# Convolution columns with the feature ahead of the distance, the ternary weights in 48 even pieces, and the squares moved to GpSimd

## What is computed

```python
# k = v = context, q = layer-normed x; 32 heads of head_dim 8, L = 512
kv = jnp.einsum('bhil,bhjl->bijhl', k_, v_)
y = jnp.fft.irfft(jnp.fft.rfft(kv, n=2*L) * jnp.fft.rfft(ssm_kernel, n=2*L), n=2*L)[..., :L]
out = y + kv * D[None, None, None, :, None]
out = jnp.einsum('bijhl,bhil->bjhl', out, q_)
...
def weight_quant(w):
    scale = 1.0 / jnp.clip(jnp.mean(jnp.abs(w)), EPS, None)
    return jnp.clip(jnp.round(w * scale), -1.0, 1.0) / scale
```

## Time and profile before

| | |
|---|---|
| median of 3 runs | 736.14 us (735.43 to 736.41) |
| the profiled execution | 736.74 us, of which its span 734.9 us |
| PE busy | 635.0 us, 86% |
| DVE busy | 556.8 us, 76% |
| ACT busy | 440.3 us, 60% |
| POOL busy | 265.3 us, 36% |
| attention | 0 to 296.3 us |
| convolution with ternary weights | 296.3 to 457 us |
| convolution without them | 457 to 489 us |
| last heads and first rows of the feed-forward part | 489 to 507 us |
| feed-forward part | 507 to 734.9 us |

### The profile page before, as it was taken

The page is one execution under the profiler, slowest core; times in us unless marked ns, Lnnn a source line. Parts: engine busy times, 40 slices in busy tenths (PEclk is TensorE's granted clock), DMA queues, the critical chain, the costliest instruction groups (busy, mean ns, idle before and its releaser), DMA issues.

```text
span 734.9 us, 10711 instructions
## 1 busy us (share of the span) xinstructions
PE 635.0 (86%) x3055; PEld 354.8 (48%) x3074; DVE 556.8 (76%) x981; ACT 440.3 (60%) x751; POOL 265.3 (36%) x248
## 2 busy tenths in 40 slices
PE   5899999999999988877778787974789999999995
PEld 3435454554545434655556565652344444444442
DVE  3465756767583644488787888999999999999983
ACT  2446675676667551666666666421676767767781
POOL 1001010000100030555554555642565655656672
PEclk9969999999999969999999999995999999999998
DMA  9535072543618150444535544220001011010001
GB/s 315 143 136 116 1 229 50 178 100 128 171 57 229 44 143 0 153 159 132 181 118 148 170 130 124 85 86 15 15 16 58 29 43 43 29 57 29 15 30 43
DMA packets 34245, 72.51 MB, mean 99 GB/s; under 512 B 4336, under 2 KB 16112, under 8 KB 32560
## 3 DMA queue, kind: packets, MB, share of 16 engines
q1 hardware_dynamic: 31056, 60.72, 28.0%
q10 hardware_dynamic: 3168, 11.54, 4.9%
HBM read 47.51 MB, written 4.28 MB: 70 GB/s over the span
## 4 chain that ended last, share of the span: by engine, by line
DVE 26%; issue 11%; ACT 9%; POOL 6%; PE 5%; ACTq 1%; DVEq 1%; POOLq 0%
POOL big L790 6%; DVE qo L758 4%; ACT wst L848 4%; DVE toep L1184 3%; DVE xq L1170 3%; DVE mb L1188 3%; PE ps L1061 2%; PE ps L1049 2%; DVE act8t L1220 2%; ACT wt L852 2%; ACT ys L829 2%; DVE x_all L1133 1%; DVE mx L1155 1%; DVE xn L1151 1%; DVE st L1138 1%
## 5 line engine op out<-in xcount | busy, mean ns | idle before, releaser
L705 PE MATMUL ps<-kv,toep 128*128 128x288 f32 x640 | 165.4, 416 | 35.5 <-DVE big L750 33.5
L705 PEld LDWEIGHTS ps<-kv,toep 128*128 128x128 f32 x640 | 121.4, 193 | 79.6 <-issue 47.7
L1061 PE MATMUL ps<-wt,xqt 128*128 128x512 bf16 x496 | 122.1, 389 | 11.1 <-DVE toep L1184 9.5
L758 DVE TENSOR_REDUCE qo<-big 128x2048 f32 (+1 forms) x32 | 124.2, 3881 | 0.0
L1313 POOL TENSOR_TENSOR big<-toep,wst 128x512 f32<-128x512 f32 x64 | 81.6, 1276 | 59.5 <-DVE toep L1184 59.4
L393 ACT ACTIVATE big<-ps,kscale 128x512 f32<-128x512 f32 x128 | 85.2, 696 | 13.6 <-PE ps L243 11.9
L243 PE MATMUL ps<-qx,kx 128*128 128x512 f32 x128 | 78.2, 639 | 11.2 <-ACT big L393 10.4
L790 POOL TENSOR_TENSOR big<-ys,qd 128x768 f32<-128x768 f32 x32 | 55.4, 1732 | 85.9 <-ACT ys L830 68.6
L1061 PEld LDWEIGHTS ps<-wt,xqt 128*128 128x128 bf16 x512 | 48.6, 100 | 67.0 <-DVE toep L1184 11.2
L747 DVE TENSOR_TENSOR big<-ps,qd 128x1024 f32<-128x1024 f32 x32 | 39.1, 1223 | 38.2 <-ACT ys L830 37.3
L1049 PE MATMUL ps<-wt,act8t 128*128 128x512 bf16 x253 | 60.8, 386 | 7.8 <-DVE act8t L1220 7.7
(11 more groups left out here) (121 smaller groups left out, 1011.8 us busy)
## 6 DMA issues: line engine op xcount, KB each, us to landing
qx<-kv SPq DMA_DIRECT2D x128, 128.0 KB, 2.4
wst<-in_wall SPq DMA_DIRECT2D x12, 1024.0 KB, 6.0
wst<-in_wall ACTq DMA_DIRECT2D x22, 512.0 KB, 4.6
toep<-krows SPq DMA_DIRECT2D x32, 256.0 KB, 3.4
ctx<-in_ctxt SPq DMA_DIRECT2D x32, 192.0 KB, 2.4
out_y<-ot SPq DMA_DIRECT2D x16, 256.0 KB, 2.0
conv_part<-qo SPq DMA_DIRECT2D x14, 256.0 KB, 2.7
x_all<-in_x SPq DMA_DIRECT2D x2, 1536.0 KB, 14.4
```

The lines of the kernel that those rows point to most:

```text
L705: mm = pe.matmul(m.ps[:, LB * r + lb, :].rearrange("p (b s) -> p b s", s=WIDE)[:, :, 0:PAIRS], m.toep[r][:, d * P:(d + 1) * P], m.kv[r][:, ...
L758: nc.vector.tensor_reduce(qo[:, :, bass.ds(h * HD, HD)], z[r].rearrange("p n s j -> p n j s"), AX.X, ALU.add).then_inc(s_red.sem, 1)
L1061: mm = pe.matmul(bank[:, n % 2, :], xqt[r][:, k, :], wt[:, k, n * C:(n + 1) * C], start=(k == 0), stop=(k == CK - 1))
```

## The change

Four things change together.

1. The columns of `kv` and so of the convolved sums are ordered with the feature first and the distance second: column 4 i + d in place of 8 d + i. POOL writes the products with a step of 4 numbers, ACT gathers with a step of 4 out of PSUM, and `z` is laid out as block[feature][shift], so that the sum reads consecutive numbers. DVE then writes runs of 4 (line 747) and single numbers with a step of 8 (line 750), and POOL writes with a step of 8 in `multiply_shifted`.
2. POOL makes the squares too: its first instruction for a head's products covers distances 0 to 3 (1024 numbers per partition in place of 768). ACT's squares are gone.
3. The weights come in 48 pieces of 512 columns, three in each of the 16 turns of two heads. In the even head's part the first piece stands between `empty` and `double`, the second behind `double`; in the odd head's the third stands between `empty` and `double`.
4. The pieces are loaded by SP, with three buffers (`wst` has four slots, of which the fourth only serves the later load of `g`). The first stage reads the same array in four pieces for each load.

```diff
-def context_products(nc, m, r, first):
+def context_products(nc, m, r):
 
     c, kv = m.ctx[r][:], m.kv[r].rearrange("p l (b s) -> p (l b) s", s=PAIRS)
-    n = HD // 2 - first
-    whole = nc.gpsimd.tensor_tensor(kv[:, :, first * HD:HD * HD // 2].rearrange("p n (d i) -> p n d i", i=HD),
-                                    window(c, 0, (CW, LB * B), (0, n), (1, HD)),
-                                    window(c, first, (CW, LB * B), (1, n), (1, HD)), ALU.mult)
...
+    n = HD // 2
+    nc.gpsimd.tensor_tensor(window(kv, 0, (PAIRS, LB * B), (1, n), (n, HD)),
+                            window(c, 0, (CW, LB * B), (0, n), (1, HD)),
+                            window(c, 0, (CW, LB * B), (1, n), (1, HD)), ALU.mult)
     return nc.gpsimd.tensor_tensor(kv[:, :, HD * HD // 2:PAIRS], c[:, :, 0:HD // 2], c[:, :, HD // 2:HD], ALU.mult)
...
-        nc.vector.tensor_tensor(z[r][:, :, 0:H, :],
-                                y[:, :, 0:H * HD].rearrange("p n (d j) -> p n d j", j=HD),
-                                window(q, 0, (2 * HD, NB), (1, H), (1, HD)), ALU.mult)
-        nc.vector.tensor_tensor(z[r][:, :, H, :].rearrange("p n (a j) -> p n a j", j=H),
+        nc.vector.tensor_tensor(z[r][:, :, :, 0:H],
+                                y[:, :, 0:H * HD].rearrange("p n (j d) -> p n j d", d=H),
+                                window(q, 0, (2 * HD, NB), (1, HD), (1, H)), ALU.mult)
+        nc.vector.tensor_tensor(z[r][:, :, :, H].rearrange("p n (a j) -> p n a j", j=H),
...
-        nc.vector.tensor_reduce(qo[:, :, bass.ds(h * HD, HD)], z[r].rearrange("p n s j -> p n j s"), AX.X, ALU.add).then_inc(s_red.sem, 1)
...
+        nc.vector.tensor_reduce(qo[:, :, bass.ds(h * HD, HD)], z[r][:], AX.X, ALU.add).then_inc(s_red.sem, 1)
...
         with sp.Fori(1, PR - 1) as i:
-            for r in range(2):
-                toeplitz(i, r)
-                context(i + 1, r)
+            toeplitz(i, 0)
+            context(i + 1, 0)
+            toeplitz(i, 1)
+            weights(i, 0)
+            weights(i, 1)
+            context(i + 1, 1)
+            weights(i, 2)
...
-            nc.gpsimd.tensor_tensor(z[r][:, :, HD - SHIFTS:HD, :],
+            nc.gpsimd.tensor_tensor(z[r][:, :, :, HD - SHIFTS:HD].rearrange("p n j s -> p n s j"),
...
-            y = sums(r)[:, :, HD:H * HD].rearrange("p n (d i) -> p n d i", i=HD)
+            y = sums(r)[:, :, 0:H * HD].rearrange("p n (i d) -> p n d i", d=H)[:, :, 1:H, :]
...
+        def turn(i, first=False):
+            for r in range(2):
+                empty(2 * i + r, r, first)
+                ternary(i, 2 * r)
+                double(2 * i + r + 2, r)
+                if r == 0:
+                    ternary(i, 1)
 
         for r in range(2):
             double(r, r, first=True)
...
+        turn(0, first=True)
+        with act.Fori(1, PR - 1) as i:
+            turn(i)
         for r in range(2):
             empty(H2 - 2 + r, r)
+        for s in range(3):
+            ternary(PR - 1, s)
```

More of the change, by code:

```diff
@@ L50 @@
 WCH = 12
+PIECES = WCH * FF // C
 LN_EPS, RMS_EPS, SUB_EPS, Q_EPS = 1e-5, 1.1920929e-07, 1e-6, 1e-5
@@ L177, in _ @@
         for r in range(2):
-            sp.dma_start(wst[:, r, :], wall[r]).then_inc(d_ws[r].sem, 16)
+            sp.dma_start(wst[:, r, :].rearrange("p (b n) -> p b n", n=C),
+                         wall[r * 4:(r + 1) * 4].rearrange("b p n -> p b n")).then_inc(d_ws[r].sem, 16)
         spread_q(1)
@@ L580, in weight_means @@
             dve.wait_ge(c_scale.sem, 1)
-            nc.vector.tensor_copy(m.wscale.rearrange("p (w k) -> p w k", w=3), spread(wrec[:], WCH // 3))
+            nc.vector.tensor_copy(m.wscale.rearrange("p (w k) -> p w k", w=3), spread(wrec[:], PIECES // 3))
         def turn(i, has_prev=True, has_next=True, rows=True):
@@ L729, in convolve @@
     qd = [sb(f"qd{r}", [P, NB, 2, HD]) for r in range(2)]
-    z = [m.big[:, (2 + r) * FF:(3 + r) * FF].rearrange("p (n i j) -> p n i j", i=HD, j=HD) for r in range(2)]
-    d_wc = [sig("d_wc0"), sig("d_wc1")]
+    z = [m.big[:, (2 + r) * FF:(3 + r) * FF].rearrange("p (n j s) -> p n j s", j=HD, s=HD) for r in range(2)]
+    d_wc = [sig(f"d_wc{s}") for s in range(3)]
     s_ys, s_qd, s_z1, s_z2, s_red = (sig(n) for n in ("s_ys", "s_qd", "s_z1", "s_z2", "s_red"))
-    s_sq = m.s_sq
     s_rnd, s_tern = sig("s_rnd"), sig("s_tern")
@@ L771, in context, with weights @@
             sp.wait_ge(m.s_kv.sem, 2 * i + r - 1)
-            sp.wait_ge(s_sq.sem, 2 * i + r - 1)
             load_context(sp, m, ctxt, 2 * i + r, r)
-        for r in range(2):
-            load_weights(sp, 0, r)
-        with sp.Fori(1, PR - 1) as i:
-            for r in range(2):
-                toeplitz(i, r)
-                context(i + 1, r)
+        def weights(i, s, first=False):
+            if not first:
+                sp.wait_ge(s_tern.sem, 3 * i + s - 2)
+            sp.dma_start(wst[:, s, :], wall[bass.ds(3 * i + s, 1)].rearrange("o p n -> (o p) n")
+                         ).then_inc(d_wc[s].sem, 16)
+        for s in range(3):
+            weights(0, s, first=True)
+        with sp.Fori(1, PR - 1) as i:
+            toeplitz(i, 0)
[5 more added lines that the diff above has]
+            weights(i, 2)
         for r in range(2):
             toeplitz(PR - 1, r)
+        for s in range(3):
+            weights(PR - 1, s)
     def gpsimd(pool):
@@ L842, in double, with ternary @@
                      ).then_inc(s_qd.sem, 1)
-        def ternary(n, r):
-            act.wait_ge(d_wc[r].sem, (n + 1) * 16)
+        def ternary(i, s):
+            n = 3 * i + s
+            act.wait_ge(d_wc[s].sem, (i + 1) * 16)
             apart(act)
-            act.activation(wst[:, r, :], wst[:, r, :], ACT.Identity, bias=m.magic[:, 0:1],
+            act.activation(wst[:, s, :], wst[:, s, :], ACT.Identity, bias=m.magic[:, 0:1],
                            scale=m.wscale[:, bass.ds(n, 1)]).then_inc(s_rnd.sem, 1)
-            act.wait_ge(s_rnd.sem, 2 * n + r + 1)
+            act.wait_ge(s_rnd.sem, n + 1)
             apart(act)
[L852 to L857, removed]
+            act.activation(wt[:, bass.ds(n, 1), :].rearrange("p o n -> p (o n)"),
+                           wst[:, s, :], ACT.Sign, bias=m.magic[:, 1:2]).then_inc(s_tern.sem, 1)
+        def turn(i, first=False):
[5 more added lines that the diff above has]
+                    ternary(i, 1)
         for r in range(2):
             double(r, r, first=True)
[L861 to L876, removed]
-                squares(2 * i + r + 2, r, i + 2)
-                double(2 * i + r + 2, r)
+        turn(0, first=True)
+        with act.Fori(1, PR - 1) as i:
+            turn(i)
         for r in range(2):
             empty(H2 - 2 + r, r)
+        for s in range(3):
+            ternary(PR - 1, s)
     def vector(dve):
@@ L1043, in down @@
         def down(t, first=False):
-            if not first:
+            if first:
+                pe.wait_ge(m.s_tern.sem, PIECES)
+            else:
                 wait(pe, s_fin, t - 1, 1)
@@ L1371, in decoder_layer @@
         m.d_toep = [Signal(ctx.enter_context(nc.semaphore(f"d_toep{r}")), 16) for r in range(2)]
-        m.s_kv, m.s_sq, m.s_conv = (Signal(ctx.enter_context(nc.semaphore(n)), 1) for n in ("s_kv", "s_csq", "s_conv"))
+        m.s_kv, m.s_conv = (Signal(ctx.enter_context(nc.semaphore(n)), 1) for n in ("s_kv", "s_conv"))
         with ExitStack() as stage:
```

28 lines of the change are left out of this document (10 added, 18 removed).

## The result

The median fell from 736.26 us (735.43 to 736.41, 4 runs) to **689.31 us** (688.91 to 690.51, 4 runs): a ratio of 0.9367, interval 0.9351 to 0.9383. The profiled execution took 688.91 us, its span 687.1.

What follows compares the result with a forecast made beforehand. Waits set the pace: a chain over ACT and POOL with weights, DVE alone without. 736.74 - 36.9 (pace over 28 heads) - 5.0 (end) = 694.8, so 695 us; this case's range 689 to 699, overall 687 to 722.

Steps and rivals of the forecast that it cites:

- the two limits: Convolution stage: with weights a chain over ACT and POOL, 7.02 us a head; without weights DVE alone, 5.54 us.
- The sum over shifts: DVE's `z` sum: reading consecutive numbers takes 2.26 us instead of 3.88, 1.62 us less for each head.
- ACT's gather: ACT's copies out of PSUM with a step: 1.33 to 2.18 us until POOL starts, middle 1.75 taken.
- the gather binds ACT: ACT's stepped copies cost the full 1.72 times and set the pace, 5.37 us a head, 704 us; chance 0.25.
- POOL's steps: POOL's writes with a step: products 1.89 to 3.25 us, 2.33 taken; `multiply_shifted` 1.73 to 2.98, 1.80 taken.
- the rival built on them: POOL's stepped writes set the pace, 5.4 us a head at a factor of 1.36; around 712 us, chance 0.17.
- broken row: POOL's writes in interrupted rows, from its product of distance 4 in runs of 4: about 2.1 ns each.
- A weight piece: One piece of 512 on ACT costs 1.33 us; of three in two heads only the one behind `double` costs.
- The three chains: ACT and POOL 4.94 us a head, POOL alone 4.64, even head's end over odd head's multiplication 5.04; pace 5.05.
- Squares: Moved from ACT to POOL: nothing gained, since ACT idled there; POOL's product instruction grows from 1.47 to 1.89 us.
- SP's loads: Weight loads moved from ACT's queue to SP's, with the Toeplitz load behind: zero effect, 1.2 us of slack.
- The end: From head 30's convolution to the feed-forward matmuls: 5.0 us less, with the load of `g` hidden by a narrow margin.

Runs made afterwards that it cites:

- the single instructions: Changed kernel followed by single DVE, ACT and POOL instructions with steps up to 8 numbers, timed alone; 738.97 us, a total that says nothing.
- the short convolution: Changed kernel without the convolution's last block of rows, 6 of 10 matmul pairs a head left; 682.82 us.
- the pieces behind `double`: Changed kernel with all three weight pieces of a turn behind `double`; 726.36 us.
- each half: Kernel before with the new column order alone, 727.76 us; changed kernel with the old column order, 712.28 us.

## Why the prediction was right, step by step

The forecast was 695 us and its own range 689 to 699; 689.31 came, at the range's lower edge. The mechanism held: the two limits fell together, and PE took their place. PE back to back needs 4.85 us a head (28 heads in 136.0 with the squares on ACT), where I took 4.89 from start to start and 4.97 with the tail; the changed kernel takes 4.92.

- **The sum over shifts** took 2.26 us, as predicted, and the second multiplication 0.63 of at most 0.7. The doubt was whether the step or the short groups cost: the single instructions settle it, 2.29 us for groups of 8 and of 32 alike, 3.8 from a step of 4 on.
- **ACT's gather was mis-sized.** I added 0.42 us to the 1.33 up to POOL's start; the copies take 0.90 and 0.40 as before. With it fell the rival *the gather binds ACT*. The rule of the Trainium skill (Advanced Engine Details and Errata, Memory Cachelines) holds for SBUF here: with lines of 16 bytes and two hits needed on each, a step of 8 bytes is free (2.29 us) and one of 16 pays (3.77). For PSUM it gives lines of 8 bytes, but what it names as slowed by scattered access are matmuls, and the prediction carried that over to ACT. ACT's copies with a step of 4, 8 and 16 bytes all take 0.799 us; the measurement decides.
- **POOL's steps** were mis-sized too, and the rival built on them fell. Its products took 2.08 us where I took 2.33, `multiply_shifted` 1.76 where I took 1.80. The Trainium skill's half as much again (GPSIMD Engine Reference, Performance pitfalls for Q7 kernels), stated for reads with a step over 8 bytes, isn't seen in writes, nor in reads of one input taken twice (1.89 us at 8 bytes, 2.02 at 32). The 2.1 ns that I took for a broken row doesn't follow from the earlier trace rows, where 0.055 us over 32 rows is 1.7 ns. With the old order the same product takes 1.89, so the new order costs it 10%; by what stays open, as single writes take 2.34 to 2.37 us whatever their step.
- **A weight piece** was under-sized: 1.61 us from `double`'s hand-over (352.52) to the copies (354.13) against 1.33, because the rounding with its scale takes 0.82 and the signs 0.72 where the earlier trace rows gave 0.63 for each. That two of three are free was right, and cost 37 us when it was undone. I named POOL's multiplication as cover, and the sum over ACT and POOL without it (12.4 us for two heads) is what came; the Toeplitz load that was late then lay in PE's idle time.
- **The three chains.** With measured values ACT and POOL need 2 x (1.33 + 1.96 + 0.52) + 1.61 = 9.2 us for two heads (9.44 with the short convolution, where these chains are the limit), POOL 2.08 + 0.46 + 1.76 + 0.1 = 4.4 a head, and the way from an even head's end over the odd head's multiplication to the convolution that waits for it 9.7 (head 6's last matmul ends at 327.83, head 9's first starts at 337.56), level with PE's 2 x 4.85. That chain leaves the 0.3 us that PE loses in four heads, and that go when POOL's product is shorter. So the pace was 4.92 instead of 5.05, 40.6 us instead of 36.9.
- **Squares** were to gain nothing: in the total they don't, and in the stage their move costs 1.6 us through POOL's longer product.
- **SP's loads** cost nothing in the changed kernel; the slack is real but small, as the pieces behind `double` show.
- **The end** gave 5.5 us for 5.0 forecast. The load of `g` stayed hidden.
- **The feed-forward's 2.4 us** I didn't foresee. 1.3 of them come up to its first output addition, 42.3 us after the first feed-forward matmul instead of 43.6. Part may be DVE, no longer behind in the first turn, and part the clock, which before fell to 0.50 there for a second time (3.4 us from 519.33); they aren't told apart. The other 1.4 are the wait ahead of an output addition near the end, and that is the clock and not the change:

```profile
720.72:724.13 3.41, 2.86 (x7) 1.04 (x8) 1.00 (x2) 1.82 (x1) 1.43 (x1) 0.50 0.00 0
726.32 0.75 DVE L1228 SCALAR_TENSOR_TENSOR ot<-ps,fd,x_all 128x512 f32<-128x512 f32 x1 [4.60 <-PE ps L1049]
```

After the change the clock stays at 1.00 there and the wait is 3.20 us. In the trace of the changed kernel's repetition it falls for 3.4 us, and the wait is 4.89.

My total was 5.5 us too high: 3.7 from the pace, 0.5 from the end and 2.4 from the feed-forward, less 0.6 by which head 2 starts later and 0.4 by which the profiled execution after lies below its median (the rest is rounding). The 1.4 us of the clock near the end are no merit of the change.

## What to carry to other kernels

When two chains limit a stage at nearly the same pace, price what each half gives alone: here 8 and 24 us, and 47 together. Put work that nothing waits for where its engine waits already, and check what stands behind it in the queue that feeds it. When PE runs back to back, read what the next chain needs (here 4.69 us a head, against PE's 4.85) before shortening PE's work.

## What the runs showed of the hardware

- The price of a step in SBUF sets in between 8 and 16 bytes: for 2048 summed numbers 2.29 us at 4 and 8 bytes, 3.77 at 16, 3.81 at 32; for ACT's copies 0.83, 0.88, 1.54 and 1.56 us for 768. Summed groups of 8 and of 32 cost the same, 2.29 us.
- ACT reads PSUM with steps of 4, 8 and 16 bytes at one price, 0.799 us for 768 numbers.
- POOL multiplies two different inputs, read in order, in 2.34 us for 1024 numbers, and one input with itself, read with steps of 8 to 32 bytes, in 1.89 to 2.02.
- At a granted clock of 0.50 seven of the convolution's matmuls took 3.4 us; at 1.00 twenty take 4.85. Such stretches of 3.4 or 6.8 us near the end come and go between traces of one kernel or of close kin, and one wait for PE's matmuls, 3.20 us without them, is 4.60 and 4.89 us behind 3.4 of such a stretch and 6.05 behind 6.8.
